# A four-layer model on one core: shorter quotient chain, split masks, transposed residuals, slot maxima split on GpSimd

## What is computed

```python
def _L1_ffn_ref(x, wg, bg, w1, b1, w2, b2, gamma, beta):
    scores = jax.nn.softmax(x @ wg + bg, axis=-1)          # 16 experts
    _, top_i = jax.lax.top_k(scores, 2)
    masked = scores * jax.nn.one_hot(top_i, E).sum(-2)
    denom = masked.sum(0, keepdims=True) + 1e-6            # over the 8 batches
    route = masked / denom * capacity                      # capacity = 8
    _, seq_ids = jax.lax.top_k(jnp.transpose(route, (2, 0, 1)), S // 2)   # 128 of 256 tokens
    ...                                                    # each expert's MLP on its tokens, added up
    z = x + outs
    return layernorm(z) * gamma + beta

def _L2_ffn_ref(x, phi_w, phi_b, expert_w, expert_b):
    logits = (jnp.einsum('tzd,ed->tze', x, phi_w) + phi_b).reshape(t, z, 64, 32)
    D = jax.nn.softmax(logits, axis=3)                     # over the 32 slots
    C = jax.nn.softmax(logits, axis=2)                     # over the 64 experts
    X_tilde = jnp.einsum('tznp,tzd->npd', D, x)
    ...                                                    # normalise, tanh, expert_w
    return jnp.einsum('tznp,npH->tzH', C, Y_tilde)
```

## Time and profile before

| what | value |
|---|---|
| median of 3 runs | 1142.11 us (1142.01 to 1143.24) |
| span of the profiled execution, first to last instruction | 1140.3 us |
| TensorE busy | 1020.7 us (90%) |
| VectorE busy | 760.8 us (67%) |
| ScalarE busy | 499.1 us (44%) |
| GpSimd busy | 154.3 us (14%) |
| mean granted TensorE clock | 0.976 of full speed |

### The profile page before, as it was taken

The page is one execution under the profiler, slowest core; times in us unless marked ns, Lnnn a source line. Parts: engine busy times, 40 slices in busy tenths (PEclk is TensorE's granted clock), DMA queues, the critical chain, the costliest instruction groups (busy, mean ns, idle before and its releaser), DMA issues.

```text
span 1140.3 us, 18292 instructions
## 1 busy us (share of the span) xinstructions
PE 1020.7 (90%) x6790; PEld 763.6 (67%) x6790; DVE 760.8 (67%) x1828; ACT 499.1 (44%) x823; POOL 154.3 (14%) x164
## 2 busy tenths in 40 slices
PE   4989999999667979999999998897799999999886
PEld 3878888888456757767767666665567666666543
DVE  5465655555384578887887878657376766768646
ACT  2255444525451444553654633231735444454251
POOL 1120110100010050000050000410021120112000
PEclk9999999999788999999999999999999999999999
DMA  8010000000030130110030000300000000000000
GB/s 333 2 29 15 15 16 15 7 9 15 1 130 1 56 129 1 57 56 26 31 129 2 1 1 1 113 1 1 1 1 6 1 6 6 1 6 1 6 6 9
DMA packets 11800, 35.39 MB, mean 31 GB/s; under 512 B 2570, under 2 KB 5818, under 8 KB 10944
## 3 DMA queue, kind: packets, MB, share of 16 engines
q1 hardware_dynamic: 10464, 33.14, 8.2%
q10 hardware_dynamic: 1152, 1.05, 0.3%
q0 software_dynamic: 96, 0.04, 0.0%
HBM read 33.16 MB, written 1.06 MB: 30 GB/s over the span
## 4 chain that ended last, share of the span: by engine, by line
issue 42%; PE 41%; DVE 7%; POOLq 3%; ACT 3%; POOL 2%; DVEq 1%; ACTq 0%
PE ps L847 5%; PE ps L1147 5%; PE ps L1122 3%; PE ps L1298 3%; PE ps L1189 2%; PE ps L881 2%; PE ps L1209 2%; PE ps L857 2%; PE ps L1229 2%; PE ps L893 2%; PE ps L904 2%; POOLq L2153 1%; POOLq L2158 1%; PE ps L836 1%; DVE arena L1956 1%
## 5 line engine op out<-in xcount | busy, mean ns | idle before, releaser
L1975 DVE TENSOR_REDUCE arena<-ps 128x8 f32<-128x2048 f32 x32 | 73.2, 2288 | 27.1 <-PE ps L1189 27.0
L1506 ACT ACTIVATE arena<-ps 128x2048 f32<-128x2048 f32 x32 | 60.1, 1877 | 50.1 <-PE ps L1213 50.0
L1033 PE MATMUL ps<-arena,uR 128*128 128x512 f32 x128 | 68.8, 620 | 8.2 <-ACT arena L1451 7.9
L1122 PE MATMUL ps<-uR,arena 128*128 128x256 f32 x256 | 73.9, 385 | 0.0
L1058 PEld LDWEIGHTS ps<-arena 128*128 128x128 f32 x512 | 61.1, 191 | 6.6 <-issue 3.0
L1058 PE MATMUL ps<-arena 128*128 128x128 f32 x512 | 63.0, 276 | 2.0 <-DVE xacc L1898 1.2
L1298 PE MATMUL ps<-arena 128*128 128x512 f32 x128 | 61.7, 606 | 2.8 <-DVE xacc L2051 1.2
L1147 PE MATMUL ps<-arena 128*128 128x256 f32 x256 | 60.6, 384 | 3.2 <-DVE arena L1929 2.6
L1479 ACT ACTIVATE arena<-ps 128x512 f32<-128x512 f32 x64 | 37.8, 597 | 51.9 <-PE ps L1123 51.7
L847 PE MATMUL ps<-arena 128*128 128x256 f32 x256 | 58.3, 386 | 0.0
L1873 DVE TENSOR_REDUCE arena<-ps 128x16 f32<-128x512 f32 x64 | 44.3, 692 | 20.2 <-PE ps L1034 15.6
(11 more groups left out here) (390 smaller groups left out, 2354.7 us busy)
## 6 DMA issues: line engine op xcount, KB each, us to landing
arena<-in_skills SPq DMA_DIRECT2D x16, 768.0 KB, 5.7
arena<-in_expert_w SPq DMA_DIRECT2D x2, 2048.0 KB, 8.3
arena<-in_l_experts SPq DMA_DIRECT2D x8, 386.5 KB, 3.2
arena<-in_consts_b SPq DMA_DIRECT2D x1, 1152.0 KB, 9.5
x2R<-in_x ACTq DMA_DIRECT2D x8, 128.0 KB, 6.5
arena<-in_L_w SPq DMA_DIRECT2D x2, 512.0 KB, 11.8
arena<-in_phiC SPq DMA_DIRECT2D x1, 1024.0 KB, 12.5
arena<-in_expert_b SPq DMA_DIRECT2D x1, 1024.0 KB, 5.0
```

What stands on the lines that cost most here:

```text
L1033: mm(high[:, c, :], uR[:, b, k * P:(k + 1) * P], phiC[:, col:col + 512], start=True, stop=False)
L1122: mm(o, phiC[:, st_ * P:(st_ + 1) * P], uR[:, b, :], start=True, stop=False)
L1506: av(pexp[:, t, gp].rearrange("p c h t -> p (c h t)"), scores[:, :, :].rearrange("p c t -> p (c t)"), ACT.Exp, scale=SCALE3).then_inc(s.sc ...
L1975: V.tensor_reduce(nm[:, k, :, 2 * gp:2 * gp + 2], scores[:, :, :].rearrange("p c (h t) -> p c h t", h=2), X, ALU.max, negate=True).then_in ...
```

## The change

Seven things change. The quotient chain splits the denominator at 32 columns, puts independent products side by side between drains, and leaves the multiply by 8 to the copy out of PSUM. Only the first batch's mask is made ahead of stage B; the other seven are steps MK in VectorE's list. The three residual matmuls with the identity become accumulating transposes. The two bf16 parts of the slot maxima are made by GpSimd in 64 steps MD, with two buffers for the maxima (nmd) and a semaphore each way (mx_ready from VectorE; md_ready on to TensorE, which VectorE also waits for before it writes a buffer again). The sum of Exp has two buffers (dsum). Some drains at the head of steps go. All engines' lists are new permutations; of these the diff shows the parts that are spoken of later.

```diff
@@ ORDER_A, "DVE": the first line, before and after
-    LN0.0 SQ.0 NH0.0 SQ.0 SQ.0 SIM.0 SIG.0 WB.0 GA0.0 GB0.0 GE0.0
+    SIG.0 WB.0 LN0.0 SQ.0 NH0.0 SQ.0 SQ.0 SIM.0 GA0.0 GB0.0 GE0.0 WF.0 LN0.1 NH0.1 S8A0.0 S8A1.0 MXA.0 GA0.1 GB0.1
...
@@ ORDER_BD, "SP"
-    LOAD.0 LOAD.1 LOAD.2 EWA.0 LOAD.3 LOAD.4 LOAD.5 LOAD.6 EWB.0 LOAD.7 EBD.0 ST.0 ST.1 ST.2 ST.3 ST.4 ST.5 ST.6 ST.7""",
+    LOAD.0 LOAD.1 LOAD.2 LOAD.3 LOAD.4 LOAD.5 LOAD.6 EWA.0 LOAD.7 EWB.0 EBD.0 ST.0 ST.1 ST.2 ST.3 ST.4 ST.5 ST.6
...
@@ ORDER_BD, "DVE": the first lines
-    BC0.0 BC1.0 LN.0 ZN.0 X2.0 BC0.1 BC1.1 SU0.0 LN.1 SU1.0 ZN.1 SU2.0 BC0.2 SU3.0 BC1.2 SU4.0 SU5.0 LN.2 X2.1 ZN.2
+    BC0.0 BC1.0 MK.1 LN.0 ZN.0 MK.2 X2.0 BC0.1 BC1.1 SU0.0 LN.1 SU1.0 ZN.1 SU2.0 SU3.0 BC0.2 MK.3 X2.1 SU4.0 BC1.2
+    SU5.0 LN.2 ZN.2 MK.4 LG0.0 LG1.0 SU0.1 X2.2 BC0.3 BC1.3 SU1.1 LG2.0 SH0.0 SU2.1 LN.3 LG3.0 SU3.1 LG4.0 ZN.3
...
@@ ORDER_BD, "POOL": up to stage D
-    RSZ.0 RSZ.1 RSZ.2 RSZ.3 W.0 W.1 WA.1 W.2 WA.2 W.3 RSZ.4 WA.3 RSZ.5 W.4 RSZ.6 RSZ.7 WA.4 W.5 WA.5 W.6 WA.6 W.7
-    JR0.0 JR1.0 WA.7 VZ.0 CSA.1 CSB.1 QM.0 CSA.2 CSB.2 QM.1 RS1.0 QM.2 CSA.3 CSB.3 RS1.1 RS2.0 QM.3 CSA.4 CSB.4 RS1.2
+    W.0 W.1 RSZ.0 RSZ.1 RSZ.2 WA.1 W.2 MD0.0 MD1.0 MD2.0 RSZ.3 MD3.0 MD4.0 MD5.0 WA.2 MD6.0 MD7.0 MD0.1 MD1.1 MD2.1
+    MD3.1 MD4.1 MD5.1 RSZ.4 MD6.1 W.3 MD7.1 MD0.2 MD1.2 MD2.2 MD3.2 MD4.2 RSZ.5 MD5.2 MD6.2 MD7.2 MD0.3 MD1.3 MD2.3
+    MD3.3 WA.3 W.4 WA.4 MD4.3 RSZ.6 MD5.3 W.5 WA.5 MD6.3 MD7.3 MD0.4 MD1.4 MD2.4 MD3.4 W.6 MD4.4 MD5.4 RSZ.7 MD6.4
+    MD7.4 MD0.5 MD1.5 MD2.5 WA.6 MD3.5 MD4.5 MD5.5 W.7 MD6.5 MD7.5 MD0.6 WA.7 MD1.6 MD2.6 MD3.6 MD4.6 MD5.6 MD6.6
...
@@ -482,6 +486,7 @@
         half_neg = neg16[:, 0:K]
         selPx = sb("selPx", [67, ST, P], BF16)
         msk = sb("msk", [P, K, NB, 16])
+        free_md = sb("nmd1", [P, 48])
 
 
         stats = per_stream("stats", [P, K, 6])
@@ -568,18 +573,19 @@
         phib = sb("phib", [P, 16])[:, :]
         phib_parts = sb("phib_parts", [P, 3, 16], BF16)
         phib_d = nc.dram_tensor("phib_scratch", (3, 2 * HALF), BF16).ap()
-        nmd = tb([P, 16])
+        nmd = [tb([P, 16]), free_md[:, 0:16]]
         nmd3 = [tb([P, P], BF16) for _ in range(2)]
         mdT = [tb([P, P], BF16) for _ in range(2)]
-        dsum = tb([P, 32])
+        dsum = [tb([P, 32]), free_md[:, 16:48]]
         nmc = tb([P, K, 4, 32])
         mcn = tb([P, K, 32])
         mc3 = tb([P, K, P], BF16)
         den = tb([P, K, 16])
         route = tb([P, K, NB, 16])
         rden = tb([P, K, 16])
-        den_hi, den_lo, q_hi, q_lo, prod, rem = (H3[1][:, a, :].rearrange("p (k b e) -> p k b e", k=K, b=NB)
-                                                 for a in range(6))
+        q_hi, q_lo, prod, prod2, prod3, rem = (H3[1][:, a, :].rearrange("p (k b e) -> p k b e", k=K, b=NB)
+                                               for a in range(6))
+        dhi, dlo = (H3[1][:, 6, 32 * a:32 * a + 32].rearrange("p (k e) -> p k e", k=K) for a in range(2))
         rR, rRb = tb([P, T]), tb([P, NB, T], BF16)
         rm8 = tb([P, 8])
         eD = [tb([P, K, HALF]) for _ in range(U)]
@@ -903,7 +909,7 @@
                             pe.wait_ge(s.hid_scaled, at(b, 2, e // 4))
                         mm(tail[:, 0:T], w0["w2"][:, e, :], S8m[u][:, e, :], start=e == 0, stop=False)
                     for k in range(K):
-                        last = mm(tail[:, k * P:(k + 1) * P], hsT[b % 3][:, k, :], ident, start=False, stop=k == K - 1)
+                        last = mm(tail[:, k * P:(k + 1) * P], hsT[b % 3][:, k, :], ident, start=False, stop=k == K - 1, is_transpose=True)
                     last.then_inc(s.moe_mm, 1)
                 for j in range(2):
                     if n == f"UG{j}":
@@ -976,7 +982,7 @@
                         for j in range(4):
                             mm(o, hid[b][:, j, k * P:(k + 1) * P], l1w2[:, j, :], start=j == 0, stop=False)
                         mm(o, rR[:, k * P:(k + 1) * P], l1b2[:, b, :], start=False, stop=False)
-                        last = mm(o, uR[:, b, k * P:(k + 1) * P], ident, start=False, stop=True)
+                        last = mm(o, uR[:, b, k * P:(k + 1) * P], ident, start=False, stop=True, is_transpose=True)
                     last.then_inc(s.z_mm, 1)
                 if n == "ZT":
                     pe.wait_ge(s.zn_ready, at(b))
@@ -1247,7 +1253,7 @@
                     pe.wait_ge(s.saC_ready, at(b))
                     for k in range(K):
                         o = low[:, 2, T + k * P:T + (k + 1) * P]
-                        mm(o, sC[u][:, k * P:(k + 1) * P], ident, start=True, stop=False)
+                        mm(o, sC[u][:, k * P:(k + 1) * P], ident, start=True, stop=False, is_transpose=True)
                         last = mm(o, saC[:, k * P:(k + 1) * P], wo3, start=False, stop=True)
                     last.then_inc(s.o_mm, 1)
                 if n == "X5T":
@@ -1782,34 +1788,35 @@
 
 
             V.reciprocal(rden, den)
+            V.tensor_scalar(dhi.bitcast(I32), den.bitcast(I32), -4096, None, ALU.bitwise_and)
             dr()
-            denw = den.unsqueeze(2).to_broadcast([P, K, NB, 16])
-            rdenw = rden.unsqueeze(2).to_broadcast([P, K, NB, 16])
+            wide_of = [P, K, NB, 16]
+            rdenw, dhiw, dlow = (a.unsqueeze(2).to_broadcast(wide_of) for a in (rden, dhi, dlo))
             V.tensor_tensor(route, msk[:, :, :, :], rdenw, ALU.mult)
-            V.tensor_copy(den_lo, denw)
+            V.tensor_tensor(dlo, den, dhi, ALU.subtract)
             dr()
             V.tensor_scalar(q_hi.bitcast(I32), route.bitcast(I32), -4096, None, ALU.bitwise_and)
-            V.tensor_scalar(den_hi.bitcast(I32), den_lo.bitcast(I32), -4096, None, ALU.bitwise_and)
             dr()
+            V.tensor_tensor(prod, q_hi, dhiw, ALU.mult)
             V.tensor_tensor(q_lo, route, q_hi, ALU.subtract)
-            V.tensor_tensor(den_lo, den_lo, den_hi, ALU.subtract)
-            V.tensor_tensor(prod, q_hi, den_hi, ALU.mult)
+            V.tensor_tensor(prod2, q_hi, dlow, ALU.mult)
             dr()
             V.tensor_tensor(rem, msk[:, :, :, :], prod, ALU.subtract)
-            for a, b in ((q_hi, den_lo), (q_lo, den_hi), (q_lo, den_lo)):
-                dr()
-                V.tensor_tensor(prod, a, b, ALU.mult)
-                dr()
-                V.tensor_tensor(rem, rem, prod, ALU.subtract)
+            V.tensor_tensor(prod3, q_lo, dhiw, ALU.mult)
+            dr()
+            V.tensor_tensor(rem, rem, prod2, ALU.subtract)
+            V.tensor_tensor(prod, q_lo, dlow, ALU.mult)
+            dr()
+            V.tensor_tensor(rem, rem, prod3, ALU.subtract)
+            dr()
+            V.tensor_tensor(rem, rem, prod, ALU.subtract)
             dr()
             V.tensor_tensor(rem, rem, rdenw, ALU.mult)
             dr()
             V.tensor_tensor(route, route, rem, ALU.add)
-            dr()
-            V.tensor_scalar(route, route, float(NB), None, ALU.mult)
             dr().then_inc(s.route_ready, 1)
             dve.wait_ge(s.route_T, 1)
-            V.tensor_copy(rR, PF[0][:, 0:T])
+            V.tensor_scalar(rR, PF[0][:, 0:T], float(NB), None, ALU.mult)
             dr()
             for i in range(T // 2 // 8):
                 V.max(rm8, rR)
@@ -1818,10 +1825,9 @@
                 if i == 3:
                     last.then_inc(s.rounds_done, 1)
                 dr()
+            V.tensor_scalar(rRb[:, 0, :], rR, 0.0, con("rowb")[:, 0:1], ALU.is_lt, ALU.mult).then_inc(s.mask_ready, 1)
+            dr()
             V.tensor_scalar(rR, rR, 0.0, None, ALU.is_lt)
-            dr()
-            for b in range(NB):
-                V.tensor_scalar(rRb[:, b, :], rR, con("rowb")[:, b:b + 1], None, ALU.mult).then_inc(s.mask_ready, 1)
             dr()
 
             low, high = PS[0], PS[1]
@@ -1834,6 +1840,8 @@
                         dve.wait_ge(s.l1_bc_mm, at(b, 2, h))
                         some = hid[b][:, 2 * h:2 * h + 2, :].rearrange("p j t -> p (j t)")
                         V.tensor_tensor(some, some, low[:, 1, :], ALU.mult).then_inc(s.l1_hid_ready, 1)
+                if n == "MK":
+                    V.tensor_scalar(rRb[:, b, :], rR, con("rowb")[:, b:b + 1], None, ALU.mult).then_inc(s.mask_ready, 1)
                 if n == "LN":
                     dr()
                     dve.wait_ge(s.z_mm, at(b))
@@ -1866,15 +1874,10 @@
                     h, k, c = st_ // 4, st_ // 2 % 2, st_ % 2
                     lg = high[:, c, :].rearrange("p (n q) -> p n q", q=PSLOT)
                     if n == f"LG{st_}":
-                        dr()
                         dve.wait_ge(s.lg_mm, at(b, 8, st_))
-                        if b == 0:
-                            dve.wait_ge(s.phib_ready, 1)
-                        V.tensor_reduce(nmd, lg, X, ALU.max, negate=True)
-                        dr()
-                        V.tensor_copy(nmd3[c][:, 0:16], nmd)
-                        dr()
```

(18 more changed lines are left out.)

237 lines of the change are left out of this document (119 added, 118 removed).

## The result

| kernel | median of 4 runs, us | lowest to highest | ratio to before, 95% interval |
|---|---|---|---|
| before | 1142.67 | 1142.01 to 1145.91 | |
| changed | 1084.24 | 1082.16 to 1086.03 | 0.9489 [0.9467, 0.9511] |

The account below looks back on a forecast made before the run. TensorE was taken to bound stages A, B and D (96, 92, 92% busy), VectorE's serial chain the junction. Terms -1.3 - 1.6 - 4.9 - 7.6 + 1.4 = -14.0 us gave 1140.3 - 14.0 + 1.8 = 1128 us, range 1115 to 1140.

Parts of the forecast that it names:

- The step that failed: All engines' lists: the other reorderings of the same steps cost nothing, sign open, 4 us either way.
- The quotient chain: Junction, VectorE: fewer drains, multiply moved into the copy out of PSUM, denominator split at 32 columns; -1.3 us.
- the masks: Junction, VectorE: only the first mask ahead of the first product, the other seven between stage-B steps; -1.6 us.
- The transposed residuals: MOE, Z and WO on TensorE: 48 tiles at 0.11 us less each, 5.3 us, at 93% share; -4.9 us.
- The slot maxima: Stage B: cast and subtraction moved from VectorE to GpSimd; -5.5 - 1.0 - 2.6 + 1.5 = -7.6 us.
- The slow matmuls: Stage B, TensorE: four matmuls after the collision wait take 2.02 us instead of 1.03; 1.0 us to be saved.
- the 4.1 us wait: Stage B: TensorE idle 4.11 us while VectorE's 16-column subtraction is held by GpSimd work from 422.45; expected to go.
- The start: Stage A: VectorE does SIG and WB before batch 0's layer norm, delaying TensorE's first large products; +1.4 us.
- VectorE did not limit B: Rival, stage B: Exp and TensorE's own order limit, freed time turns idle; 1136 us, chance 0.20.
- VectorE holds GpSimd: Rival, stage B: VectorE's normalising multiplies hold back GpSimd's pairs by about 0.95 us each; 1142 us, no change, chance 0.09.
- GpSimd's queue: Rival, stage B: eleven weight products between the pairs make them late and TensorE waits; 1161 us, slower, chance 0.11.
- the forecast's sign of being wrong: TensorE's MT waits for GpSimd over 5 us, a VectorE reduce waiting for GpSimd, or stage B unshortened with gaps at Exp.

Follow-up runs that it names:

- the nine places: All edits with the old lists, nine single TensorE steps moved between SH and the LG behind it in stage B, against the edits with old lists (1126.74): 1124.96 us.
- the corners: All edits, old or new step orders in stages B and D: both old 1126.74, new D only 1108.29, new B only 1103.47, both new 1084.24 us.
- two swaps: Kernel before with two neighbouring VectorE steps exchanged twice (SA0 and SA1 of batch 0 ahead of MX0 and MX1 of batch 1): 1144.81 us, ratio 1.0002.

## Why the prediction was wrong, step by step

**The step that failed** is the sentence "The other permutations of the same steps I cost at nothing: TensorE has the same work at the same share; the sign is open, 4 us either way". The permutations are worth 33.9 us alone and 42.5 with the edits. The step takes TensorE's share of 92% as given, but the share is what the order sets. The same rows hold the measure that I should have used: 29.4 us idle in B and 30.4 in D, some 60 us that an order may give back (and it can add to them). It is no strict bound, as 10.3 us of B's 30.7 came out of TensorE's shown busy time. Of these some 1.5 are Z's transposes, some 1.4 the 26 missing records, and an estimated 2.4 a stretch at half clock (last section); the rest isn't traced to single instructions. The range, besides, took in only 2 of the 4 us.

**The quotient chain and the masks**: right, -1.45 and -1.64 us for -1.3 and -1.6.

**The transposed residuals**: price right (0.11 us for one tile), and in stage B the size too (1.5 of 1.8 us). Whether the whole is 4.9 is open: the medians give 2.4 with overlapping ranges. By the four-fold price of the Trainium skill ("TensorE: Matmul & The Clock Gate", Terms) a tile would take 0.055 us, an estimate; the trace shows 0.11.

**The slot maxima**: with the old lists the sum came out near, the ways did not. Stage B lost 8.1 us, Z's at most 1.8 us in it, for a forecast of 7.6. That is partly luck: only 2.5 of the 8.1 are idle time of TensorE, and with the old lists no run has the slot maxima alone (drains, dsum and masks changed in B too). TensorE's waits for the parts fell only from 7.5 to 5.0 us, since they passed to GpSimd, and those for Exp didn't fall at all (7.9 to 8.6), where a third was to go. The slow matmuls behind the 4.1 us wait were put at 1.0; their price was rather 2.4 (last section). And what ran on GpSimd at 422.45 is WA, the sum, not a product. With the new lists the same move is worth 21.2 us.

**The start**: no run shows the +1.4 us; what batch 0 loses is made up before the junction or lies below what the runs can tell.

**Sum of the edits**: without the start's +1.4 the forecast was -15.4, and the edits alone with the old lists give -15.0. After what is said of its terms, that nearness is in part luck.

**The rivals.** "VectorE did not limit B" holds for the old lists in its mechanism (the waits for Exp stayed), not in its time. "VectorE holds GpSimd" fell: no pair was held (197 to 200 ns), and GpSimd stood idle before 60 of the 64 pairs, waiting for VectorE's reduce (the other four ran right behind other work of GpSimd: three powers and a weight sum). "GpSimd's queue" fell as well, with the new lists: without the products the time is the same. With the old lists TensorE did wait 5.0 us for GpSimd, once for 2.5, just at the forecast's sign of being wrong (over 5 us). The Trainium skill ("Perfetto Trace Analysis", Optimizing Scalar/DVE Operations) warns that moving work between VectorE and GpSimd might not help because they share a port. Here it helped by 21 us: the parts are small (0.20 and 0.22 us on GpSimd), and the products and sums that collided with them are now in the same queue.

**What stays open.** In stage B, which moves give the 19 us or so that the nine places don't explain. A list of one engine alone wasn't tried, as each new list is laid out for the others' new order. So what the lists gain as a whole is shown by the corners (B's 22.6 us of stage length, at most 3.6 of it by single moves); that they gain by fitting each other is not shown.

## What to carry to other kernels

Where engines walk fixed lists, price a re-ordering by the idle time of the bounding engine in each stage, never at nothing, and look first at the stage that is filling. Here the new order gave 15 us for 17.5 idle in the fill, and for 29.9 idle in B 11.6 alone and 22.6 with the edits. Mending one wait at a time mostly moved it to the next (two swaps gave nothing that can be told, nine moves 1.8 us); relieving an engine paid in full only with an order that let the relief through (15.0 and 33.9 us apart, 58 together). When a trace shows several waits with different releasers in one stage, add them all up: removing one group alone handed the time to the others here.
